# A Mamba-2 and mixture-of-experts block on one core: two gate pairs of in-projection done in the group's own first scan tile

## Chip, core and metric

The kernel runs on one core of one Trainium2 chip, written at the level of the engines' own instruction streams. The metric is device time in microseconds (us) of one execution. One core has TensorE (matmuls), VectorE, ScalarE, GpSimd and SyncE, which here only issues DMAs; each runs its own instructions in order, and semaphores tie them together.

## The reference

The input is 2048 tokens of 512 numbers. A layer norm is followed by two branches whose results are added to the input: a Mamba-2 block and a mixture of 8 experts with the top 2 taken.

```python
xn = _layernorm(x)
zxbcdt = xn @ in_proj_w.T                     # 1024 z, 1280 xBC, 16 dt
xBC = silu(conv_b + sum(conv_w[:, k] * xp[:, k:k + l, :] for k in range(4)))
...                                           # scan over chunks with decays exp(dt * A)
y = (Y_diag + Y_off) + x_heads * D_skip
y = y * silu(z)
y = y * rsqrt(mean(y * y) + EPS) * norm_w
out = x + y @ out_proj_w.T + moe(xn)
```

The gate z enters at one place only: after the scan has given y, y is multiplied by silu(z). The columns xBC are needed from the first step of the scan.

## The kernel before

The experts run first (the trace's first 300 us or so, with layer norm and routing ahead of them); the Mamba part follows. Its 16 tiles of 128 tokens (t = 0 to 15) are scanned one after the other, and two tiles make one group of 256 tokens (g = t // 2; c = t % 2 is the tile's place in it, so "even" tiles have c = 0 and "odd" ones c = 1).

**In-projection** works on a whole group at a time, in 9 pairs of column blocks: `PAIRS` (L150) names five pairs that go through the convolution (`True`) and four gate pairs, the z pairs (`False`). A pair is 24 matmuls of 128 by 256 into one of two PSUM banks, `pi[n % 2]` (`stage_pe`, L1323). A conv pair is then copied to `raw` by ScalarE, which also makes the first tap (`stage_act`, L1262); VectorE adds three taps to each of its two blocks, six instructions (L1297), and after a tanh on ScalarE finishes the pair with one instruction (L1309), which stands in the code of the next pair. A z pair is one tanh on ScalarE (L1278) and one instruction on VectorE (L1303). TensorE may write a bank again when its last reader is done: ScalarE's copy for a conv pair, VectorE's L1303 for a z pair.

**Order.** Group 0's nine pairs are done in a lead-in ahead of tile 0. After that group g + 1's pairs are spread over the two tiles of group g: `TAKEN` (L943) puts pairs 0 to 3 in the even tile and 4 to 8 in the odd one. Group 7 has no group behind it, so tiles 14 and 15 have no pairs.

**A tile on TensorE**: transposes of the tile's x (L1629, L1633), a pair (`stage(0)`), a product for C and B (L1637, behind ScalarE's `btok` copy), a pair (`stage(1)`), the out-projection of the tile before (`project(t - 1)`, 16 matmuls at L1593, and then the sum of squares at L1598, which waits for GpSimd's tree of sums), the first half of the carried state's product (`off(0)`, L1614), a pair (`stage(2)`), `off(1)`, half of the tile's own product (`diag(0)`, L1621), the state update (L1655), `diag(1)`, and what pairs are left (`stage(3)`, `stage(4)`).

**A tile on VectorE**: `xdt` (two instructions, L1494), `cbm` (L1501), the masking of `m` (L1504, 2048 elements), `dec` (L1447) for the next tile, the residual of the tile before, the conv or gate work of the tile's first two pairs, the variance and `decayed(0)` (L1467), the output of the tile before (L1567), `decayed(1)`, `own(0)` (L1476), the third pair's work, the split of x in odd tiles (L1320), `own(1)`, `carry` (L1533), and then the work of the remaining pairs.

**ScalarE and GpSimd** are tied to it so: `dec` on VectorE lets ScalarE do its exponentials (L1360, L1361), four parts of `m` (L1368), and then the square of y of the tile before (L1384); behind that square GpSimd makes the tree of three sums (L1206 to L1210) for which L1598 waits. GpSimd also adds and gates y at a tile's end (L1252, L1255) and makes `xdd` when `xdt` is there (L1226).

All engines run group 0 unrolled, groups 1 to 6 in a loop of two groups a turn, and group 7 unrolled.

Of the kernel before, what the change touches and what calls it, by code (L numbers as in the profile page):

```python
# [36 lines left out]
G = T // 2  # L37
# [107 lines left out]
CR = 1  # L145
# [1 line left out]
SLOT = 2 * GU + 2 * DW  # L147


PAIRS = ((True, 0), (True, 1), (True, 2), (False, 0), (True, 3), (True, 4), (False, 1), (False, 2), (False, 3))  # L150
NP = len(PAIRS)
EARLY = XB * D * 4 + KD * GT * 4 + 384


# [34 lines left out]
def static(i, *values):  # L189
    return isinstance(i, int) and i in values  # L190
# [747 lines left out]
def mamba(nc, low, over, late, wraw, whl, wo, xh0, smalls, hooks, sem, x, w_in, w_out_in, conv_w_in, conv_b_in,  # L938
# [1 line left out]
    NX, NZ = CB // 2, XB // 2  # L940
    y_out, y_done, down, h_lo = experts.y_out, experts.y_done, experts.down, experts.h_lo
    assert NP == NX + NZ
    TAKEN = ((0, 1, 2, 3), (4, 5, 6, 7, 8))  # L943
    with ExitStack() as ctx:
        def pb(name, shape):
            return ctx.enter_context(nc.psum_tensor(name, shape, F32))
# [40 lines left out]
        w_lo = sem("w_lo")  # L987
# [145 lines left out]
        def sync(sp):  # L1133
            sp.wait_ge(down, J + CR)
            sp.wait_ge(y_done, J + CR)
            sp.wait_ge(h_lo, J + 2)
            for i in range(2):
                sp.wait_ge(y_out[i], 16 * ((J + 1 - i) // 2) + 16)

            def load_x(g, par):  # L1140

                sp.dma_start(xl[par][:, :, :].bitcast(F32), xt_d[g]).then_inc(xg_in[par], 16)

            def load_decays(t, c):
                sp.dma_start(m[c][:, :, :], cs_d[t].unsqueeze(0).broadcast_to([P, HEADS, P])).then_inc(bc_in[c], 16)

            def load_decays2(t):
                for half in range(2):
                    sp.dma_start(e2[half * HD:(half + 1) * HD, :, :],
                                 cs_d[t][half * XB:(half + 1) * XB, :].unsqueeze(0).broadcast_to([HD, XB, P])  # L1150
                                 ).then_inc(e2_in, 16)

            def store(t):
                sp.wait_ge(o_done, t + 1 + CR)
                sp.dma_start(out_t[t], o[:, :]).then_inc(o_out, 16)

            sp.wait_ge(w_lo, NP)
            load_decays(0, 0)
            load_x(1, 1)

            def body(g, par):
                for c in range(2):
                    t = g * 2 + c
                    if not static(t, T - 1):
                        sp.wait_ge(ydiag, t * 2 + CR)
                        load_decays(t + 1, 1 - c)
                    if c == 0 and not static(g, G - 2, G - 1):
                        sp.wait_ge(in_full, g * NP + NP + CR)
                        load_x(g + 2, par)
                    elif c == 0 and static(g, G - 2):  # L1170

                        sp.wait_ge(in_full, g * NP + NP + CR)
                        sp.sem_inc(xg_in[par], 16)
                    sp.wait_ge(yadd, t + CR)
                    load_decays2(t)
                    if not static(t, 0):
                        store(t - 1)
                    sp.dma_start(res[:, :], x_t[t]).then_inc(res_in, 16)

            body(0, 0)  # L1180
            body(1, 1)
            with sp.Fori(0, (G - 4) // 2) as i:
                body(i * 2 + 2, 0)
                body(i * 2 + 3, 1)
            body(G - 2, 0)
            body(G - 1, 1)
            store(T - 1)
            sp.wait_ge(o_out, 16 * T + 16)
# [157 lines left out]
        def scalar(act):  # L1346
# [36 lines left out]
                act.wait_ge(ygate, t + 1 + CR)  # L1383
                act.activation(ysq[:, :, :], y[:, :, :], ACT.Square).then_inc(ysqd, 1)  # L1384

            for n in range(NP):
                stage_act(act, 0, n, 0)
                if n == 6:
                    decay_factors(0, 0)
            split_act(act, 1, 1, 0)  # L1390
            kernel_part(0, 0, 0, 1)
# [1 line left out]
            def body(g, par, r):  # L1393
                for c in range(2):
                    t = g * 2 + c
                    taken = TAKEN[c] if not static(g, G - 1) else ()
                    more = not static(t, T - 1)
                    act.wait_ge(btr, t + 1)
                    act.wait_ge(st, t + CR)
                    act.copy(btok[:, :], pk[:, 0, :]).then_inc(btok_done, 1)  # L1400
                    for n in taken[:1]:
                        stage_act(act, g + 1, n, 1 - par)
                    act.wait_ge(e2_in, t * 32 + 32)
                    act.activation(e2[:, :, :], e2[:, :, :], ACT.Exp).then_inc(e2_done, 1)
                    if more:
                        decay_factors(t + 1, 1 - c)
                        kernel_part(t + 1, 1 - c, 0, 4)
                    if not static(t, 0):
                        square(t - 1)
                    for n in taken[1:2]:  # L1410
                        stage_act(act, g + 1, n, 1 - par)
                    if more:
                        kernel_part(t + 1, 1 - c, 1, 4)
                        kernel_part(t + 1, 1 - c, 2, 4)
                    for n in taken[2:3]:
                        stage_act(act, g + 1, n, 1 - par)
                    if more:
                        kernel_part(t + 1, 1 - c, 3, 4)
                    if c == 1 and taken:
                        split_act(act, g + 2, par, r + 1)  # L1420
                    for n in taken[3:]:
                        stage_act(act, g + 1, n, 1 - par)

            by_twos(act, G, body)
            square(T - 1)
# [1 line left out]
        def vector(dve):  # L1427
# [18 lines left out]
                dve.wait_ge(cst_done, t + 1)  # L1446
                dve.tensor_tensor(dec[c][:, :], m[c][:, :, P - 1], cst[c][:, :], ALU.subtract).then_inc(dsub, 1)  # L1447

            for n in range(NP):
                stage_dve(dve, 0, n, 0)  # L1450
                if n == 6:
                    decay_differences(0, 0, 0)
            split_dve(dve, 1, 1)

            def body(g, par):
                for c in range(2):
                    t = g * 2 + c
                    tok = slice(c * P, (c + 1) * P)
                    first = static(t, 0)
                    taken = TAKEN[c] if not static(g, G - 1) else ()  # L1460

                    def decayed(half):

# [43 lines left out]
                        decay_differences(t + 1, g + c, 1 - c)  # L1507
                    if not first:
                        residual(t - 1)
                    for n in taken[:2]:  # L1510
                        stage_dve(dve, g + 1, n, 1 - par)
                    if static(t, T - 1):
                        decayed(0)
                    if not first:
# [4 lines left out]
                        finish(t - 1)  # L1519
                    decayed(1)  # L1520
                    own(0)
                    for n in taken[2:3]:
                        stage_dve(dve, g + 1, n, 1 - par)
                    if c == 1 and taken:
                        split_dve(dve, g + 2, par)
                    own(1)
# [3 lines left out]
                    for half in range(2):  # L1530
# [1 line left out]
                        sl = carry[:, 4 * half:4 * half + 4, :, :].rearrange("p b a d -> p (b a d)")  # L1532
                        dve.tensor_tensor(sl, pxb[half][:, :, :].rearrange("p b l -> p (b l)"), sl,  # L1533
                                          ALU.add).then_inc(cadd, 1)
                    for n in taken[3:4]:
                        stage_dve(dve, g + 1, n, 1 - par)
                    for n in taken[4:]:
                        stage_dve(dve, g + 1, n, 1 - par)

            def residual(t):  # L1540

# [33 lines left out]
        def tensor(pe):  # L1575
            for s in (st, yoff, ydiag, op, ss):
                pe.sem_inc(s, CR)
            for n in range(1, NP):
                pe.wait_ge(w_lo, n + 1)
                stage_pe(pe, 0, n, 0)  # L1580
            pe.wait_ge(prep, 5)
            pe.wait_ge(wo_done, XB)

# [16 lines left out]
            def body(g, par):  # L1600
                for c in range(2):
                    t = g * 2 + c
                    tok = slice(c * P, (c + 1) * P)
                    taken = TAKEN[c] if not static(g, G - 1) else ()

                    def stage(n):
                        for k in taken[n:n + 1]:
                            stage_pe(pe, g + 1, k, 1 - par)

                    def off(half):  # L1610
                        pe.wait_ge(ye, t * 2 + half + CR)
# [108 lines left out]
```

## Time and profile before

| | us |
|---|---|
| median of 3 runs | 784.98 (784.42 to 787.63) |
| the profiled execution | 790.81, span 789.0 |
| TensorE busy | 670.8 (85% of the span) |
| VectorE busy | 527.7 (67%) |
| ScalarE busy | 379.9 (48%) |
| GpSimd busy | 310.6 (39%) |
| lead-in's last matmul until tile 1's x transposes | 328.35 to 355.68 |
| tiles 2 to 13 | 384.3 to 726.5 |
| tiles 14 and 15 | 726.5 to 789.0 |

Times in rows are microseconds from the start of the span. A group of rows on one engine, in order of time, has the start, the length, the engine, the line of the kernel, the operation, the names written and read, and the count; brackets hold the idle time of the engine just before, and the instruction that ended it. PEclk is the clock granted to TensorE as a share of the full one: 1.00 is 2.4 GHz and 0.50 is 1.2 GHz.

### The profile page before, as it was taken

The numbers are of one execution on the slowest core, as the hardware profiler recorded it, in microseconds if no ns is written. First come the engines' busy times: TensorE is split into PE (matmuls) and PEld (weight loads), VectorE is DVE, ScalarE is ACT, GpSimd is POOL, SyncE is SP. The second block draws the span as 40 slices with busy tenths as digits, with TensorE's granted clock in tenths as the row PEclk, the third lists the DMA queues.
The fourth block names the chain that finished last, engine by engine and source line by source line (L and its number), as shares of the span: only waits on it lengthen the run. The fifth ranks groups of instructions, "written<-read, shape, count | busy, mean of one in ns | idle before, by whom it ended". The sixth has DMA issues, their size and how long they took to land.

```text
span 789.0 us, 13831 instructions
## 1 busy us (share of the span) xinstructions
PE 670.8 (85%) x4176; PEld 532.2 (67%) x4177; DVE 527.7 (67%) x1051; ACT 379.9 (48%) x776; POOL 310.6 (39%) x288
## 2 busy tenths in 40 slices
PE   0555446999999987979999999899999899999765
PEld 0233225999999877867877786686787687777432
DVE  4676682443444467678788788678788778787453
ACT  3333112444554465676557466456556546564410
POOL 3345103222222200126465464464555455556441
PEclk9866756999999998999999999999999999999797
DMA  8788102654456623212432343242243242134120
GB/s 246 269 283 287 53 7 70 185 187 120 141 180 178 237 101 147 68 61 65 144 117 63 116 134 99 63 134 83 78 132 107 56 131 106 53 107 133 54 64 29
DMA packets 36072, 96.47 MB, mean 122 GB/s; under 512 B 5376, under 2 KB 9216, under 8 KB 33856
## 3 DMA queue, kind: packets, MB, share of 16 engines
q1 hardware_dynamic: 28304, 67.96, 25.0%
q0 software_dynamic: 7728, 28.05, 13.0%
q8 instruction: 16, 0.26, 0.1%
q14 instruction: 24, 0.20, 0.1%
HBM read 73.06 MB, written 22.94 MB: 122 GB/s over the span
## 4 chain that ended last, share of the span: by engine, by line
PE 51%; issue 15%; DVE 12%; POOL 10%; DMA 7%; ACT 3%; POOLq 0%; DVEq 0%; SPq 0%; ACTq 0%
PE pi L1341 17%; PE pg L879 10%; PE pd L890 6%; PE py L1614 4%; PE po L1593 3%; PE py L1621 3%; DMA xn_d<-xin 3%; DMA xin<-in_x 2%; PE px L864 2%; POOL y L1252 2%; POOL ysq L1206 2%; DVE y L1476 2%; POOL xdd L1226 2%; PE pxb L1655 2%; DVE xs L1297 1%
## 5 line engine op out<-in xcount | busy, mean ns | idle before, releaser
L1341 PE MATMUL pi<-xh,whl 128*128 128x256 f32 x1152 | 169.2, 291 | 9.0 <-ACT raw L1272 4.5
L1341 PEld LDWEIGHTS pi<-xh,whl 128*128 128x128 f32 x1152 | 150.7, 194 | 13.4 <-issue 7.1
L1297 DVE SCALAR_TENSOR_TENSOR xs<-raw,conv_w,xs 128x256 f32<-128x256 f32 x240 | 119.5, 567 | 4.6 <-ACT xs L1275 4.6
L1593 PE MATMUL po<-wo,y 128*128 128x512 f32 x256 | 114.9, 602 | 1.9 <-POOL y L1255 1.9
L1341 PE MATMUL pi<-xl,whl 128*128 128x256 f32 x576 | 93.5, 285 | 0.0
L1593 PEld LDWEIGHTS po<-wo,y 128*128 128x128 f32 x256 | 48.2, 193 | 57.6 <-issue 55.3
L1341 PEld LDWEIGHTS pi<-xl,whl 128*128 128x128 f32 x576 | 79.8, 193 | 0.0
L1368 ACT ACTIVATE m<-m,cst 128x128 f32<-128x128 f32 x256 | 79.4, 388 | 0.5
L879 PE MATMUL pg<-ew,xgh 128*128 x312 | 65.3, 352 | 0.0
L1252 POOL TENSOR_TENSOR y<-y,e 128x1024 f32<-128x1024 f32 x15 | 35.9, 2390 | 66.6 <-DVE y L1476 66.6
L1226 POOL TENSOR_TENSOR xdd<-xdt,dec 128x1024 f32<-128x1024 f32 x15 | 29.1, 1938 | 72.7 <-DVE xdt L1494 72.7
L1206 POOL TENSOR_TENSOR ysq<-ysq 128x512 f32<-128x512 f32 x16 | 22.6, 1412 | 86.4 <-ACT ysq L1384 78.6
L879 PEld LDWEIGHTS pg<-ew,xgh 128*128 128x128 f32 x312 | 53.5, 192 | 0.3
L765 POOL COPY ic<-idx 128x1 uint32 (+1 forms) x39 | 7.2, 183 | 115.3 <-PE px L864 79.1
L1504 DVE TENSOR_TENSOR m<-m,cbm 128x2048 f32<-128x2048 f32 x16 | 51.1, 3194 | 1.7
L768 POOL DMA_INDIRECT xg<-xn_d,ic x39 | 38.1, 977 | 31.7 <-POOL ic L765 31.7
L1278 ACT ACTIVATE zs<-pi 128x512 f32<-128x512 f32 x32 | 19.1, 598 | 63.4 <-PE pi L1341 63.4
L649 PE MATMUL pt<-ident,xin 128*128 128x128 f32 x64 | 15.7, 427 | 39.5 <-DVE xin L423 39.5
L1239 POOL DMA_INDIRECT ya<-y_d,sidx x32 | 40.1, 1254 | 18.0 <-POOL sidx L1234 13.2
L832 DVE SCALAR_TENSOR_TENSOR hg<-th,pg 128x192 f32<-128x192 f32 x39 | 13.8, 354 | 49.9 <-ACT th L788 49.9
L890 PE MATMUL pd<-ew,hh 96*128 x156 | 45.8, 414 | 0.3 <-issue 0.3
L1275 ACT ACTIVATE xs<-raw,conv_b,conv_w 128x256 f32<-128x256 f32 x80 | 43.7, 594 | 1.3
(193 smaller groups left out, 1270.5 us busy)
## 6 DMA issues: line engine op xcount, KB each, us to landing
m<-cs_d SPq DMA_DIRECT2D x16, 1024.0 KB, 4.8
y_d<-yo SPq DMA_DIRECT2D x39, 256.0 KB, 3.3
e<-cs_d SPq DMA_DIRECT2D x32, 256.0 KB, 4.1
gur<-in_w_gu POOLq DMA_DIRECT2D x8, 768.0 KB, 5.2
xin<-in_x SPq DMA_DIRECT2D x8, 512.0 KB, 4.9
xn_d<-xin SPq DMA_DIRECT2D x8, 512.0 KB, 4.8
xt_d<-xt SPq DMA_DIRECT2D x8, 512.0 KB, 3.6
xl<-xt_d SPq DMA_DIRECT2D x8, 512.0 KB, 3.7
```

Source lines behind the costliest of these rows:

```text
L879: mm = pe.matmul(pg[par][:, :], xx[par][:, k, :], of(ww, e, k), start=n == 0, stop=n == 11)
L890: mm = pe.matmul(pd[par][:, :], xx[par][:, k, :], of(ww, e, k), start=n == 0, stop=n == 5)
L1206: pool.tensor_tensor(ysq[:, 0:4, :], ysq[:, 0:4, :], ysq[:, 4:8, :], ALU.add).then_inc(tree, 1)
L1226: pool.tensor_tensor(xdd[:, :, :, :], xdt[:, :, :, :], dec[c][:, :].rearrange("p (a b) -> p b a", a=2).unsqueeze(3) .broadcast_to([P, XB, ...
L1239: pool.indirect_dma_start(ya[n][:, :], None, y_d, bass.IndirectOffsetOnAxis(ap=sidx[:, n:n + 1], axis=0)).then_inc(ya_in[n], 16)
L1252: pool.tensor_tensor(y[:, :, :], y[:, :, :], e2[:, :, :], ALU.add).then_inc(yadd, 1)
L1275: act.activation(xs[par][:, b, :], raw[:, b, 0:GT], ACT.Identity, bias=conv_b[:, b:b + 1], scale=conv_w[:, b, 0:1]).then_inc(tap, 1)
L1297: dve.scalar_tensor_tensor(out=xs[par][:, b, :], in0=raw[:, b, k:k + GT], scalar=conv_w[:, b, k:k + 1], in1=xs[par][:, b, :], op0=ALU.mult ...
L1341: mm = pe.matmul(pi[n % 2][:, h, :], whl[:, n, lo, k, h * P:(h + 1) * P], xx[:, k, :], start=k3 == 0, stop=k3 == 11)
L1368: act.activation(m[c][:, h, :], m[c][:, h, :], ACT.Relu, bias=cst[c][:, h:h + 1], scale=-1.0).then_inc(seg, 1)
L1504: dve.tensor_tensor(m[c][:, :, :], m[c][:, :, :], cbm[:, :].unsqueeze(1).broadcast_to([P, HEADS, P]), ALU.mult).then_inc(m_done, 1)
L1593: mm = pe.matmul(po[:, :], y[:, b, :], wo[:, b, :], start=b == 0, stop=b == XB - 1)
```

## The change

`PAIRS` now has the five conv pairs first (0 to 4) and the four z pairs last (5 to 8). The last two, `OWN = 2`, are no longer done a group ahead: pairs 7 and 8 of group g are done in tile 2g, in the places `stage(0)` and `stage(1)`. Behind them in the same tile come pairs 0, 1, 2 of group g + 1, and pairs 3, 4, 5, 6 in the odd tile. The lead-in does 7 pairs, and tile 14 has group 7's pairs 7 and 8. On SyncE the next x for the split is loaded after the decays `e2` and no longer before, since all nine pairs of the group are now done only in its first tile.

```diff
-PAIRS = ((True, 0), (True, 1), (True, 2), (False, 0), (True, 3), (True, 4), (False, 1), (False, 2), (False, 3))
+PAIRS = ((True, 0), (True, 1), (True, 2), (True, 3), (True, 4), (False, 0), (False, 1), (False, 2), (False, 3))
+OWN = 2
...
-    TAKEN = ((0, 1, 2, 3), (4, 5, 6, 7, 8))
+    def taken_in(g, c):
+        own = [(g, n) for n in range(NP - OWN, NP)] if c == 0 else []
+        ahead = [(g + 1, n) for n in ((0, 1, 2) if c == 0 else (3, 4, 5, 6))] if not static(g, G - 1) else []
+        return own + ahead
...
+                    sp.wait_ge(yadd, t + CR)
+                    load_decays2(t)
                     if c == 0 and not static(g, G - 2, G - 1):
                         sp.wait_ge(in_full, g * NP + NP + CR)
                         load_x(g + 2, par)
...
-                    sp.wait_ge(yadd, t + CR)
-                    load_decays2(t)
...
-            for n in range(NP):
+            for n in range(NP - OWN):
                 stage_dve(dve, 0, n, 0)
-                if n == 6:
+                if n == 5:
                     decay_differences(0, 0, 0)
...
-                    taken = TAKEN[c] if not static(g, G - 1) else ()
+                    taken = taken_in(g, c)
...
-                    for n in taken[4:]:
-                        stage_dve(dve, g + 1, n, 1 - par)
+                    for of, n in taken[4:]:
+                        stage_dve(dve, of, n, par if of is g else 1 - par)
...
-            for n in range(1, NP):
+            for n in range(1, NP - OWN):
                 pe.wait_ge(w_lo, n + 1)
                 stage_pe(pe, 0, n, 0)
+            pe.wait_ge(w_lo, NP)
```

The other uses of `taken` change in the same way on ScalarE, VectorE and TensorE, and ScalarE's lead-in like VectorE's.

VectorE, from the end of tile 0 (the carry) to the first instructions of tile 1; `zs` is a z pair, `xs<-raw` are conv taps, `xs<-tx` finishes a conv pair. Before:

```order
L1533 TENSOR_TENSOR carry<-pxb,carry 128x512 x2
L1303 SCALAR_TENSOR_TENSOR zs_163<-zs_163,pi 128x512
L1309 SCALAR_TENSOR_TENSOR xs_161<-tx_178,xs_161 128x512
L1494 TENSOR_TENSOR xdt<-pxb,dt_tok 128x512 x2
L1501 TENSOR_TENSOR cbm<-pk,tri 128x128
```

and of the change:

```order
L1541 TENSOR_TENSOR carry<-pxb,carry 128x512 x2
L1305 SCALAR_TENSOR_TENSOR xs_161<-raw,conv_w,xs_161 128x256 x6
L1317 SCALAR_TENSOR_TENSOR xs_161<-tx_178,xs_161 128x512
L1305 SCALAR_TENSOR_TENSOR xs_161<-raw,conv_w,xs_161 128x256 x6
L1317 SCALAR_TENSOR_TENSOR xs_161<-tx_179,xs_161 128x512
L1502 TENSOR_TENSOR xdt<-pxb,dt_tok 128x512 x2
L1509 TENSOR_TENSOR cbm<-pk,tri 128x128
```

Two whole conv pairs now stand between the carry of an even tile and `xdt` of the odd one, where one z instruction and the finish of a conv pair stood; it is the same in tiles 2, 4, ..., 12.

TensorE in the same place, from `diag(1)` of tile 0 to the transposes of tile 1; four rows of `pi` are one pair. Before:

```order
L1621 MATMUL py<-m_151,xdt 64x128 x8
L1341 MATMUL pi<-xh_180,whl 128x256 x8
L1341 MATMUL pi<-xl_157,whl 128x256 x4
L1341 MATMUL pi<-xh_180,whl 128x256 x8
L1341 MATMUL pi<-xl_157,whl 128x256 x4
L1629 MATMUL pk<-ident,xs_160 128x128
L1633 MATMUL pxb<-ident,xs_160 128x128 x8
```

and of the change:

```order
L1630 MATMUL py<-m_151,xdt 64x128 x8
L1349 MATMUL pi<-xh_180,whl 128x256 x8
L1349 MATMUL pi<-xl_157,whl 128x256 x4
L1349 MATMUL pi<-xh_180,whl 128x256 x8
L1349 MATMUL pi<-xl_157,whl 128x256 x4
L1349 MATMUL pi<-xh_180,whl 128x256 x8
L1349 MATMUL pi<-xl_157,whl 128x256 x4
L1349 MATMUL pi<-xh_180,whl 128x256 x8
L1349 MATMUL pi<-xl_157,whl 128x256 x4
L1638 MATMUL pk<-ident,xs_160 128x128
L1642 MATMUL pxb<-ident,xs_160 128x128 x8
```

The even tile ends with two pairs where it ended with one; the odd tile has four in all where it had five.

## Rows read from the trace of the kernel before

**Rows 1.** The page, part 1: busy time, share of the span, instructions.
```profile
PE 670.8 (85%) x4176; PEld 532.2 (67%) x4177; DVE 527.7 (67%) x1051; ACT 379.9 (48%) x776; POOL 310.6 (39%) x288
```

**Rows 2.** Busy time by stretch: lead-in, tiles 2, 3, 6 and 14.
```profile
core 0: us, PE busy (x) PEld busy (x) DVE busy (x) ACT busy (x) POOL busy (x), PEclk, DMA share, GB/s
311.00:328.40 17.40, 17.40 (x147) 17.40 (x146) 13.06 (x29) 9.49 (x18) 0.00 (x0) 0.99 0.02 9
384.23:410.55 26.32, 25.89 (x180) 20.13 (x178) 21.27 (x44) 16.00 (x35) 12.68 (x11) 1.00 0.35 106
410.55:440.00 29.45, 28.97 (x203) 22.85 (x202) 24.31 (x43) 16.78 (x35) 17.52 (x13) 1.00 0.32 104
...
495.75:526.50 30.75, 27.84 (x179) 21.49 (x177) 23.54 (x44) 16.44 (x36) 13.08 (x11) 0.94 0.32 97
726.53:750.24 23.71, 19.02 (x84) 11.75 (x82) 11.19 (x18) 9.78 (x23) 10.97 (x10) 0.78 0.24 67
```

**Rows 3.** TensorE in tile 3: start, length, instruction, [idle before <-who].
```profile
411.16 1.09 PE L1633 MATMUL pxb<-ident,xs 128*128 128x128 f32 x8 [0.34 <-DVE carry L1533]
...
418.00 7.03 PE L1593 MATMUL po<-wo,y 128*128 128x512 f32 x16
425.17 0.38 PE L1598 MATMUL pk<-ones,ysq 128*128 128x1 f32 x2
```

**Rows 4.** VectorE, tiles 2, 3 and 4, the same columns.
```profile
409.82 1.28 DVE L1533 TENSOR_TENSOR carry<-pxb,carry 128x512 f32<-128x512 f32 x2
...
411.98 0.93 DVE L1309 SCALAR_TENSOR_TENSOR xs<-tx,xs 128x512 f32<-128x512 f32 x1
412.83 1.27 DVE L1494 TENSOR_TENSOR xdt<-pxb,dt_tok 128x512 f32<-128x512 f32 x2
...
415.76 3.45 DVE L1504 TENSOR_TENSOR m<-m,cbm 128x2048 f32<-128x2048 f32 x1
...
419.32 0.18 DVE L1447 TENSOR_TENSOR dec<-m,cst 128x16 f32<-128x16 f32 x1
...
421.26 6.52 DVE L1297 SCALAR_TENSOR_TENSOR xs<-raw,conv_w,xs 128x256 f32<-128x256 f32 x12
...
461.49 2.46 DVE L1297 SCALAR_TENSOR_TENSOR xs<-raw,conv_w,xs 128x256 f32<-128x256 f32 x6
```

**Rows 5.** ScalarE, tile 3, the same columns.
```profile
421.09 1.04 ACT L1384 ACTIVATE ysq<-y 128x1024 f32<-128x1024 f32 x1
```

**Rows 6.** GpSimd, tile 3, the same columns.
```profile
412.52 2.63 POOL L1255 TENSOR_TENSOR y<-y,zs 128x1024 f32<-128x1024 f32 x1 [0.17 <-POOL y L1252]
415.11 1.95 POOL L1226 TENSOR_TENSOR xdd<-xdt,dec 128x1024 f32<-128x1024 f32 x1
...
424.60 0.52 POOL L1210 TENSOR_TENSOR ysq<-ysq 128x128 f32<-128x128 f32 x1
```

**Rows 7.** Conv taps of tile 3 by line: xcount, ns min/median/max.
```profile
L1297 DVE SCALAR_TENSOR_TENSOR xs<-raw,conv_w,xs x12: 472/478/1493, 421.3 to 427.3; 128x256 f32<-128x256 f32 x12
```

**Rows 8.** VectorE and ScalarE, lead-in and tile 0.
```profile
312.55 2.56 DVE L1297 SCALAR_TENSOR_TENSOR xs<-raw,conv_w,xs 128x256 f32<-128x256 f32 x6 [0.70 <-ACT xs L1275]
...
330.11 1.23 DVE L1320 TENSOR_TENSOR xl<-xl,xh 128x1024 fp32r<-128x1024 f32 x1 [0.25 <-ACT xh L1315]
...
336.61 0.25 ACT L1400 COPY btok<-pk 128x128 f32<-128x128 f32 x1
```

**Rows 9.** TensorE after an idle time: tiles 0, 1, 6 and 14.
```profile
331.39 1.61 PE L1341 MATMUL pi<-xh,whl 128*128 128x256 f32 x8 [1.90 <-DVE xl L1320]
...
347.06 1.16 PE L1614 MATMUL py<-xs,carry 128*128 128x128 f32 x8 [3.16 <-DVE e L1467]
...
355.68 1.09 PE L1633 MATMUL pxb<-ident,xs 128*128 128x128 f32 x8 [0.39 <-DVE carry L1533]
...
512.34 0.38 PE L1598 MATMUL pk<-ones,ysq 128*128 128x1 f32 x2 [2.14 <-POOL ysq L1210]
...
739.07 0.58 PE L1598 MATMUL pk<-ones,ysq 128*128 128x1 f32 x2 [3.42 <-POOL ysq L1210]
```

More of the change, by code:

```diff
@@ L1400, in body @@
                     act.copy(btok[:, :], pk[:, 0, :]).then_inc(btok_done, 1)
-                    for n in taken[:1]:
-                        stage_act(act, g + 1, n, 1 - par)
+                    for of, n in taken[:1]:
+                        stage_act(act, of, n, par if of is g else 1 - par)
                     act.wait_ge(e2_in, t * 32 + 32)
@@ L1409, in body @@
                         square(t - 1)
-                    for n in taken[1:2]:
-                        stage_act(act, g + 1, n, 1 - par)
+                    for of, n in taken[1:2]:
+                        stage_act(act, of, n, par if of is g else 1 - par)
                     if more:
@@ L1414, in body @@
                         kernel_part(t + 1, 1 - c, 2, 4)
-                    for n in taken[2:3]:
-                        stage_act(act, g + 1, n, 1 - par)
+                    for of, n in taken[2:3]:
+                        stage_act(act, of, n, par if of is g else 1 - par)
                     if more:
@@ L1420, in body @@
                         split_act(act, g + 2, par, r + 1)
-                    for n in taken[3:]:
-                        stage_act(act, g + 1, n, 1 - par)
+                    for of, n in taken[3:]:
+                        stage_act(act, of, n, par if of is g else 1 - par)
             by_twos(act, G, body)
@@ L1447, in decay_differences @@
                 dve.tensor_tensor(dec[c][:, :], m[c][:, :, P - 1], cst[c][:, :], ALU.subtract).then_inc(dsub, 1)
-            for n in range(NP):
+            for n in range(NP - OWN):
                 stage_dve(dve, 0, n, 0)
-                if n == 6:
+                if n == 5:
                     decay_differences(0, 0, 0)
@@ L1459, in body @@
                     first = static(t, 0)
-                    taken = TAKEN[c] if not static(g, G - 1) else ()
+                    taken = taken_in(g, c)
                     def decayed(half):
@@ L1509, in body @@
                         residual(t - 1)
-                    for n in taken[:2]:
-                        stage_dve(dve, g + 1, n, 1 - par)
+                    for of, n in taken[:2]:
+                        stage_dve(dve, of, n, par if of is g else 1 - par)
                     if static(t, T - 1):
@@ L1521, in body @@
                     own(0)
-                    for n in taken[2:3]:
-                        stage_dve(dve, g + 1, n, 1 - par)
+                    for of, n in taken[2:3]:
+                        stage_dve(dve, of, n, par if of is g else 1 - par)
                     if c == 1 and taken:
@@ L1534, in body @@
                                           ALU.add).then_inc(cadd, 1)
-                    for n in taken[3:4]:
-                        stage_dve(dve, g + 1, n, 1 - par)
-                    for n in taken[4:]:
-                        stage_dve(dve, g + 1, n, 1 - par)
+                    for of, n in taken[3:4]:
+                        stage_dve(dve, of, n, par if of is g else 1 - par)
+                    for of, n in taken[4:]:
+                        stage_dve(dve, of, n, par if of is g else 1 - par)
             def residual(t):
@@ L1603, in body @@
                     tok = slice(c * P, (c + 1) * P)
-                    taken = TAKEN[c] if not static(g, G - 1) else ()
+                    taken = taken_in(g, c)
                     def stage(n):
-                        for k in taken[n:n + 1]:
-                            stage_pe(pe, g + 1, k, 1 - par)
+                        for of, k in taken[n:n + 1]:
+                            stage_pe(pe, of, k, par if of is g else 1 - par)
                     def off(half):
```

## Prediction

> **What bounds the kernel.** The page first: TensorE is busy for 670.8 of 789.0 us [rows 1]. Busy time by stretch says where the rest lies. In the steady part (tiles 2 to 13) TensorE has nothing to give: tile 2 is 26.32 us long and 25.89 busy, tile 3 29.45 and 28.97, at a granted clock of 1.00; tile 6, with one longer wait, 30.75 and 27.84 at 0.94; tile 14, without pairs, 23.71 and 19.02 at 0.78 [rows 2]. So a pair moved out of the steady part, or into idle time of tile 0 or tile 14, is worth up to its own length: in the lead-in 147 matmuls took 17.40 us, so the 24 of a pair take 24 x 17.40 / 147 = 2.84 us [rows 2]. TensorE's work is the same in sum before and after. The question is what the new order does to its waits.
>
> The second thing to read is how late the other engines are. In tile 3 (T = 410.55, its first transpose) `project` starts at 418.00 and lasts 7.03 us, to 425.03, and the sum of squares behind it starts at 425.17 [rows 3]. What releases that one is a chain over three engines: `xdt` on VectorE at 412.83, the masking of `m` from 415.76, `dec` done at 419.32 + 0.18 = 419.50 [rows 4]; the square on ScalarE at 421.09 [rows 5]; GpSimd's tree, whose last sum ends at 424.60 + 0.52 = 425.12 [rows 6]. GpSimd ends 0.05 us ahead of the matmul that waits for it. So the odd tiles hold two limits that are level: TensorE's own order and the chain xdt, m, dec, square, tree. The chain has 425.12 - 419.50 = 5.62 us from the end of `dec` to the end of the tree.
>
> **What the change gains.** (a) Lead-in. TensorE has two pairs fewer, 5.68 us, but tile 0 also needs the five conv pairs finished, which now come in a row. VectorE's third starts at 312.55 and takes 2.56 [rows 8] plus some 0.6 for a finish; three of these, a z and a finish end at 312.55 + 3 x 3.1 + 1.2 = 323.1. TensorE is done at 322.7, so tile 0 starts at about 323.1 and not 328.35: 5.2 us. (b) Tile 0 gives most of it back. ScalarE's copy `btok`, at 336.61 now [rows 8], comes some 4.5 us earlier, 332.1; pair 8 is behind it on TensorE, and pair 0 of the next group, which writes the same bank, waits for VectorE to read pair 8, behind the masking of `m`, at about 338.9. From there 3 pairs (8.52), off, diag, state update and diag (4.9) and about 1 us for half rate lead to 353.3, where tile 1 starts at 355.3 now (355.68 less its wait of 0.39, [rows 9]): 2.0 us are left. (c) From tile 1 to tile 13 seven odd tiles lose a pair and six even ones gain one: -2.84. (d) Tile 14 takes two pairs. There TensorE waited 3.42 us for the tree and then ran at half rate [rows 9]. With the pairs, `cbm` and `m` come 2.2 us later and the tree ends at about 14.5 us into the tile, as `project` does (it starts at 7.5, lasts 7.0); without the idle time I take the rest at full rate, 6.8 us, so 21.3 in place of 23.71: -2.4. Together -2.0 - 2.84 - 2.4 = -7.2 us.
>
> **What it costs in each odd tile.** Pairs 1 and 2, both conv pairs, are the last things an even tile does on TensorE, and their VectorE work stands ahead of `xdt` of the odd tile. Where `xdt` starts at T + 2.3 now [rows 4], it needs:
> The low end: pair 2's last matmul is at T, its copy and first activation let VectorE begin at T + 1.3; six taps 2.46 [rows 4] and the finish 0.6 give T + 4.4. That holds if pair 1 costs nothing.
> The high end: pair 1's taps can begin at T - 1.5, and GpSimd gates y of the even tile from about T - 1.0 to T + 1.4 (2.4 us; it comes earlier against T since the even tile is a pair longer). Taps and finish read two SBUF tensors, and they stall under a GpSimd tensor operation: one tap took 1493 ns against a median of 478 [rows 7], a finish took 0.93 under the gate, and the masking of `m` 3.45, and ended 2.15 us behind the end of `xdd`, which had started first [rows 4, 6]. If the gate holds the taps to its end, four taps of pair 1 follow it: 1.4 + 1.9 = T + 3.3, finish 3.95, six taps 6.45, finish 7.1, and with a tap that is in the way of the gate, T + 7.3.
> Between the ends: twelve taps took 6.52 us over a tree of about 2.9 us, and two sixes alone would be 4.92, so 1.6 of 2.9 was lost; by this share the gate costs 1.3 and not 2.4, and `xdt` starts at about T + 6.3. I take T + 7.3, since the 1.45 us sum, the longest of that tree, blocked a single tap for 1.0 and the gate is longer than it.
>
> The Trainium skill, page "SBUF — State Buffer", section "Who interferes with whom", says that VectorE with two SBUF inputs and a GpSimd instruction that reads SBUF exclude each other for a whole instruction, and the one that comes second is blocked. By that rule the gate costs its full 2.4 us, the high end; the 1493 ns tap agrees.
>
> From `xdt` on: 1.3 us, then `xdd` 1.95, which holds `m`, 2.15 more for `m`, 0.35 for `dec`, 5.62 to the end of the tree: 11.4 in all, so T + 18.7. TensorE, with no wait at its transposes, is through `project` at T + 0.1 + (425.03 - 411.16) = T + 14.0. It waits 4.7 us, against 0.5 and 0.1 at the transposes and the sum of squares now: +4.1. Behind it come off(0) and a pair, 3.8 us, and off(1), which needs VectorE's decayed(0). VectorE, with residual (1.75), twelve taps (6.7) and now two finishes after `dec`, reaches that at about T + 23.3: at full rate TensorE waits 0.8 more. If the idle time lowers the clock, that stretch takes some 1.7 us longer instead: waits of 1.90, 2.14 and 3.42 were followed by matmuls at half rate, one of 3.16 was not [rows 9]. I take +0.8. So +4.9 per odd tile and, from a slightly later start of the even tiles' xdt, 0.1 per even one. Seven odd tiles (1 to 13): 34.3, six even ones: 0.6.
>
> ScalarE has the same instructions as before, with `btok` behind a tanh that waits for pair 1's taps: it is there at about T + 4.0, just when TensorE comes to L1637: nothing. SyncE: the wait for the nine pairs, in the middle of the even tile now, holds back the load of x, which is split a tile later, and behind it the store, which waits for `o` longer anyway: nothing; the `e2` load no longer stands behind it, and its exponential is not on the chain. DMA traffic is the same.
>
> **The sum.** 34.3 + 0.6 - 7.2 = +27.7 us. The profiled execution took 790.81 us, 5.8 above the median of the runs; on it this gives 818.5, and on the median of 784.98 it gives 812.7. I forecast 812.
>
> **Rivals.**
> 1. The stall is small: `xdt` at T + 4.4, the low end. The tree ends at T + 15.8, TensorE waits 1.9 (+1.3), and 0.5 more at off(1): 7 x 1.8 + 0.6 - 7.2 = +6.0, 791. For it: the wait is too short to cost clock. Against it: it needs the gate not to disturb six taps.
> 2. Faster: the chain does not bind at all, and only the -7.2 is left: 778. It decides at `xdt` by T + 2.6 (14.0 less 11.4); pair 2's own six taps alone forbid that by 1.8 us unless TensorE has some other slack in the odd tile. Against it too: the chain is level with TensorE today.
> 3. The clock: a wait of 4.7 us is followed by more than one stretch at half rate, as in tile 14 (0.78 over the tile, [rows 2]). Then each odd tile costs 1.7 us more: 824.
> 4. No difference: rival 1 with a smaller wait, the seven odd tiles costing 1 us each: 785.
>
> **How the numbers follow.** Forecast 0.55, rival 1 0.20, rival 3 0.08, rival 2 0.09, rival 4 0.08. The range reaches from rival 1 to rival 3 and leaves out rivals 2 and 4, 0.17: 790 to 826. About 0.5% is what a measurement of this kernel can tell from no change: faster 0.09, within it 0.08, slower 0.83.
>
> **What will show it.** In the changed profile: tile 1 starts near 353; in every odd tile up to 13 TensorE is idle by 4 to 5 us ahead of the sum of squares, released by GpSimd; `xdt` of odd tiles starts 7 us after the first transpose; a group (even and odd tile) takes about 60.5 us where it takes 55.8; tile 14 is near 21.3 us at a granted clock near 1. I would be wrong if VectorE's taps at the tile's edge ran undisturbed (a wait under 2 us), if the odd tile's chain hid behind TensorE, or if the half rate came in most tiles and for long.

## The result: 3.2% slower, 810.6 us

| | before | after |
|---|---|---|
| median of 4 runs, us | 784.7 (780.3 to 787.6) | 810.63 (806.38 to 812.38) |
| ratio | | 1.0319, 95% interval 1.0272 to 1.0365 |
| profiled execution, us | 790.81, span 789.0 | 806.38, span 804.7 |
| start of tile 0 | 328.35 | 314.97 |
| tile 2, tile 3 | 26.32, 29.45 | 29.40, 32.56 |
| tile 4, tile 5 | 26.20, 29.37 | 29.33, 31.74 |
| tile 6, tile 10 | 30.30, 30.62 | 30.16, 30.12 |
| tile 14 | 23.71 | 21.78 |

812 was forecast. In the profiled execution of the changed kernel the part ahead of the Mamba lead-in, which the change doesn't touch, took 7.87 us less (the lead-in's third pair starts at 297.92, before at 305.79). So I compare from there on: the lead-in and the tiles took 23.6 us longer (15.7 by the spans, and 7.9), where the working had 27.7. Executions over 1.5% behind a kernel's fastest are left out of the ratios below but not of the medians (with the shorter gate they are three of ten, and its median without them is 791.93).

Busy time by stretch, the columns as in [rows 2]: the end of the lead-in, tiles 2, 3, 5, 6 and 14.

```profile
297.92:314.97 17.05, 16.59 (x120) 16.42 (x121) 16.06 (x38) 11.02 (x20) 0.00 (x0) 0.86 0.47 166
376.11:405.51 29.40, 28.63 (x204) 22.87 (x203) 18.88 (x35) 14.98 (x33) 17.47 (x13) 1.00 0.38 125
405.51:438.07 32.56, 28.54 (x179) 22.46 (x178) 28.58 (x53) 17.87 (x37) 10.82 (x11) 0.90 0.23 70
467.40:499.14 31.74, 27.57 (x179) 21.49 (x178) 28.64 (x53) 17.85 (x37) 10.86 (x11) 0.95 0.22 66
499.14:529.30 30.16, 28.92 (x204) 22.81 (x202) 19.67 (x35) 15.00 (x33) 17.51 (x13) 1.00 0.38 124
745.00:766.78 21.78, 20.23 (x131) 14.28 (x129) 12.65 (x22) 10.87 (x25) 13.57 (x11) 1.00 0.30 92
```

Tile 3 has a pair less than before (179 matmuls, where [rows 2] has 203) and takes 3.1 us longer; it is the worst of the odd tiles, the other six up to 13 take 2.1 to 2.4 us longer at clocks of 0.95. TensorE is idle for 4 us of it, and its clock is at half rate for part of the rest. TensorE in tile 3 (T = 405.51):

```profile
412.83 7.03 PE L1602 MATMUL po<-wo,y 128*128 128x512 f32 x16
423.72 0.59 PE L1607 MATMUL pk<-ones,ysq 128*128 128x1 f32 x2 [3.86 <-POOL ysq L1218]
424.17 2.06 PE L1623 MATMUL py<-xs,carry 128*128 128x128 f32 x8
425.88 2.05 PE L1349 MATMUL pi<-xh,whl 128*128 128x256 f32 x8
427.73 1.05 PE L1349 MATMUL pi<-xl,whl 128*128 128x256 f32 x4
428.59 1.28 PE L1349 MATMUL pi<-xh,whl 128*128 128x256 f32 x8
...
430.18 1.05 PE L1623 MATMUL py<-xs,carry 128*128 128x128 f32 x8
```

The sum of squares, which followed the out-projection at once in [rows 3], waits 3.86 us for GpSimd's last sum; in the other odd tiles up to 13 it is 3.67 to 3.92. Behind it eight matmuls of a pair take 2.05 us, and 1.28 and less once the clock is back. VectorE and GpSimd over the same edge say why the sum is late:

```profile
404.11 4.59 DVE L1305 SCALAR_TENSOR_TENSOR xs<-raw,conv_w,xs 128x256 f32<-128x256 f32 x6 [1.49 <-ACT xs L1283]
408.62 0.68 DVE L1317 SCALAR_TENSOR_TENSOR xs<-tx,xs 128x512 f32<-128x512 f32 x1
409.23 2.45 DVE L1305 SCALAR_TENSOR_TENSOR xs<-raw,conv_w,xs 128x256 f32<-128x256 f32 x6
411.60 0.68 DVE L1317 SCALAR_TENSOR_TENSOR xs<-tx,xs 128x512 f32<-128x512 f32 x1
412.20 1.27 DVE L1502 TENSOR_TENSOR xdt<-pxb,dt_tok 128x512 f32<-128x512 f32 x2
...
417.89 0.18 DVE L1455 TENSOR_TENSOR dec<-m,cst 128x16 f32<-128x16 f32 x1
...
427.52 0.67 DVE L1475 TENSOR_TENSOR e<-py,e 128x512 f32<-128x512 f32 x1
```

```profile
404.06 2.38 POOL L1263 TENSOR_TENSOR y<-y,zs 128x1024 f32<-128x1024 f32 x1 [0.17 <-POOL y L1260]
413.70 1.93 POOL L1234 TENSOR_TENSOR xdd<-xdt,dec 128x1024 f32<-128x1024 f32 x1 [7.26 <-DVE xdt L1502]
...
423.16 0.51 POOL L1218 TENSOR_TENSOR ysq<-ysq 128x128 f32<-128x128 f32 x1
```

Pair 1's six taps take 4.59 us and pair 2's 2.45. The first six began at 404.11, 0.05 us after GpSimd's gate. The six by line (ns minimum, median, maximum) show that one of them, of 2616 ns, paid for all of it; it ended 0.29 us behind the gate:

```profile
L1305 DVE SCALAR_TENSOR_TENSOR xs<-raw,conv_w,xs x6: 472/472/2616, 404.1 to 408.2; 128x256 f32<-128x256 f32 x6
```

So `xdt` starts at T + 6.7, where it stood at T + 2.3 [rows 4], and the tree ends at 423.67, 11.5 us behind the start of `xdt`.

### The profile page after: what moved, and what is told of

The parts are those of the page before. It is cut to its first block, busy times and chain, and to the rows that moved or that the text cites. A ratio compares the mean times of both kernels' runs of the same rounds, so it can differ in the third digit from the quotient of the medians.

```text
span 804.7 us, 13829 instructions
## 1 busy us (share of the span) xinstructions
PE 672.9 (84%) x4176; PEld 537.5 (67%) x4177; DVE 534.2 (66%) x1051; ACT 379.8 (47%) x776; POOL 300.1 (37%) x288
## 4 chain that ended last, share of the span: by engine, by line
PE 45%; issue 18%; DVE 15%; POOL 7%; ACT 6%; DMA 6%; DVEq 0%; POOLq 0%; ACTq 0%; SPq 0%
PE pi L1349 14%; PE pg L880 9%; PE pd L891 6%; PE po L1602 3%; DVE xs L1305 3%; PE py L1623 3%; DMA xin<-in_x 2%; DMA xn_d<-xin 2%; PE px L865 2%; POOL ysq L1214 2%; POOL xdd L1234 2%; ACT m L1376 2%; PE py L1630 2%; PE pxb L1664 2%; DVE xs L1317 1%
## 5 line engine op out<-in xcount | busy, mean ns | idle before, releaser
L1349 PE MATMUL pi<-xh,whl 128*128 128x256 f32 x1152 | 175.4, 298 | 5.0 <-ACT raw L1280 4.5
L1349 PEld LDWEIGHTS pi<-xh,whl 128*128 128x128 f32 x1152 | 156.9, 202 | 7.9 <-issue 7.7
L1305 DVE SCALAR_TENSOR_TENSOR xs<-raw,conv_w,xs 128x256 f32<-128x256 f32 x240 | 125.1, 586 | 12.5 <-ACT xs L1283 12.4
L1349 PE MATMUL pi<-xl,whl 128*128 128x256 f32 x576 | 95.8, 290 | 0.0
L1349 PEld LDWEIGHTS pi<-xl,whl 128*128 128x128 f32 x576 | 82.3, 199 | 0.0
L1512 DVE TENSOR_TENSOR m<-m,cbm 128x2048 f32<-128x2048 f32 x16 | 57.2, 3575 | 1.7
L1255 POOL TENSOR_TENSOR carry<-carry,cd 128x1024 f32<-128x1024 f32 x15 | 29.0, 1934 | 36.6 <-PE py L1623 36.6
L650 PE MATMUL pt<-ident,xin 128*128 128x128 f32 x64 | 14.7, 405 | 32.4 <-DVE xin L424 32.4
```

What stands on the lines that cost most here:

```text
L1305: dve.scalar_tensor_tensor(out=xs[par][:, b, :], in0=raw[:, b, k:k + GT], scalar=conv_w[:, b, k:k + 1], in1=xs[par][:, b, :], op0=ALU.mult ...
L1349: mm = pe.matmul(pi[n % 2][:, h, :], whl[:, n, lo, k, h * P:(h + 1) * P], xx[:, k, :], start=k3 == 0, stop=k3 == 11)
L1512: dve.tensor_tensor(m[c][:, :, :], m[c][:, :, :], cbm[:, :].unsqueeze(1).broadcast_to([P, HEADS, P]), ALU.mult).then_inc(m_done, 1)
```

## Experiments

The theory: conv taps ahead of the odd tile's `xdt` are the loss, the gate makes them worse, and the half rate after the wait is a part of its own. Rivals: the loss comes from doing gate pairs in their own tile; or the half rate costs nothing, since VectorE is late for `off(1)` anyway. Times are medians; ratios are against the runs of the kernel before in the same series (784.2 to 785.4).

### The own gate pairs last in the even tile

```diff
-        return own + ahead
+        return ahead + own
```

with the waits for banks and for the group's last pair set to the new order.

> The change is kept (two gate pairs of a group are done in its own even tile, the lead-in has 7 pairs, tile 14 has two), but within the even tile the order is turned round: pairs 0, 1, 2 of the next group stand in the first three places, and the group's own gate pairs 7 and 8 come last. So no convolution taps stand ahead of xdt of the odd tile, only two gate pairs. My theory (the loss is the late xdt of odd tiles, because two conv pairs with their taps stand ahead of it): the wait of 3.9 us ahead of the sum of squares falls below 1 us in odd tiles, the half rate behind it is gone, odd tiles take 29.4 less 2.84 = 26.6 us and not 31.75, so 7 x 5.1 = 36 us less than the change's own 810, less what tile 14 loses: about 775 to 782 us, faster than the kernel before. Rival (the loss comes from doing gate pairs in the group's own tile at all, by the banks or the masking ahead of L1311): it stays at 800 to 812 us.

809.15 us, ratio 1.0346 (1.0274 to 1.0418): the time is in the rival's range (800 to 812). The trace says otherwise. VectorE in tile 5 (T = 472.48):

```profile
473.92 1.28 DVE L1516 TENSOR_TENSOR xdt<-pxb,dt_tok 128x512 f32<-128x512 f32 x2
...
483.12 0.18 DVE L1466 COPY cst<-cs_tok 128x16 f32 x1 [2.60 <-DMA m<-cs_d]
483.33 0.18 DVE L1469 TENSOR_TENSOR dec<-m,cst 128x16 f32<-128x16 f32 x1
```

SyncE's queue in the same tile:

```profile
472.83 0.35 SPq L1158 DMA_DIRECT2D xl<-xt_d  x1
473.38 1.15 SPq L1171 DMA_DIRECT2D out<-o  x1
474.72 0.34 SPq L1194 DMA_DIRECT2D res<-in_x  x1
475.34 0.33 SPq L1161 DMA_DIRECT2D m<-cs_d  x1
475.77 1.15 SPq L1165 DMA_DIRECT2D e<-cs_d  x2
```

`xdt` was early, at T + 1.4, as the theory had it. But SyncE waits for the group's last pair before it loads the next x, and this pair was now at the even tile's very end. The loads of the decays stood behind that wait, were issued at 475.34 and 475.77, and `dec` waited 2.60 us for the one at 475.34 (in tile 13, where no x is loaded any more, the exponential on ScalarE waited 2.51 us for the `e` load instead). My edit had taken one wait away and made another, on a queue that I had not looked at.

### The same, with the x load behind the decays on SyncE

```diff
                         load_decays(t + 1, 1 - c)
                     sp.wait_ge(yadd, t + CR)
                     load_decays2(t)
-                    if c == 0 and not static(g, G - 2, G - 1):
+                    if c == 1 and not static(g, G - 2, G - 1):
                         sp.wait_ge(in_full, full_at(g, NP - 1) + CR)
                         load_x(g + 2, par)
```

> As the kernel with the own gate pairs last in the even tile, with one more move: SyncE's wait for the group's nine pairs and the load of the next x behind it stand in the odd tile, behind the loads of the decays, and no longer in the even tile ahead of them. In that kernel's trace the odd tiles' xdt was early (T + 1.4 in tile 5), but dec then waited 2.60 us for the load of the decays, which SyncE issued only when pair 8 was done, and in tile 13 the exponential ahead of dec's waited 2.5 us for the e2 load. Theory (the taps cost was gone and a late DMA issue had taken its place): odd tiles wait under 1 us ahead of the sum of squares and take 26.6 to 27.7 us in place of 27.7 to 33.4, so 7 x 4 us less than 809: 775 to 785 us. Rival (the loads are late because of their own traffic, or another wait of that order comes up): odd tiles stay above 29 us and the time above 795.

773.57 us, ratio 0.9861 (0.9804 to 0.9919), so faster than the kernel before. Tiles 4, 5 and 6, then TensorE in tile 5 (T = 458.22):

```profile
429.12:458.22 29.10, 28.89 (x203) 22.90 (x202) 23.34 (x46) 16.59 (x36) 16.78 (x12) 1.00 0.31 102
458.22:484.72 26.50, 26.02 (x179) 19.95 (x178) 22.62 (x41) 16.12 (x34) 12.84 (x11) 1.00 0.34 101
484.72:515.10 30.38, 29.14 (x204) 22.80 (x203) 24.52 (x46) 16.61 (x36) 16.61 (x12) 1.00 0.32 104
```

```profile
472.22 0.38 PE L1621 MATMUL pk<-ones,ysq 128*128 128x1 f32 x2
472.46 1.14 PE L1637 MATMUL py<-xs,carry 128*128 128x128 f32 x8
...
476.75 1.16 PE L1637 MATMUL py<-xs,carry 128*128 128x128 f32 x8 [0.34 <-DVE e L1489]
```

The odd tiles take 26.4 to 26.5 us: the 29.4 of before less one pair of 2.84. The even tiles take 29.1 us, the 26.2 of before and one pair. So gate pairs in their own tile, at the even tile's end, cost no more than their own length. In the places of the change, `stage(0)` and `stage(1)`, they were not run without the conv pairs at the tile's end; its even tiles are 0.2 us longer than these.

### One part of the change alone: the order of PAIRS

The kernel before with the new `PAIRS` line and nothing else of the change, groups 1 to 6 written out.

> The kernel before, groups 1 to 6 written out, with one part of the change alone: PAIRS in the new order (five conv pairs first, then four gate pairs). All nine pairs stay one group ahead, 0 to 3 in the even tile and 4 to 8 in the odd one, so nothing is done in the group's own tile, and TensorE has the same work in each tile as before. What changes is that the even tile ends with a conv pair (3) and not a gate pair. Theory (conv taps ahead of the odd tile's xdt are the cost, one pair of them a part of it): xdt of odd tiles moves from T + 2.3 to between T + 4.8 (six taps of 2.46 us and a finish behind pair 3's activation, undisturbed) and T + 7.1 (held by GpSimd's gate, which stands at T + 1.9 to T + 4.6), TensorE waits 2 to 4.5 us ahead of the sum of squares, and seven odd tiles cost 2 to 6 us each: 792 to 818 us against 778 of the written-out kernel before. Rival (the loss needs the gate pairs done in their own tile): 776 to 781.

814.31 us, ratio 1.0339 (1.0285 to 1.0392), against 778.08 for the written-out kernel before (below): 36 us (the two are from different series, whose kernels before are 1.0 us apart) for a change of order that leaves the number of pairs in each tile as it was. VectorE and GpSimd in tile 5 (T = 475.36):

```profile
476.81 4.81 DVE L1297 SCALAR_TENSOR_TENSOR xs<-raw,conv_w,xs 128x256 f32<-128x256 f32 x6 [0.86 <-ACT xs L1275]
...
482.15 1.28 DVE L1495 TENSOR_TENSOR xdt<-pxb,dt_tok 128x512 f32<-128x512 f32 x2
```

```profile
477.30 2.46 POOL L1255 TENSOR_TENSOR y<-y,zs 128x1024 f32<-128x1024 f32 x1
```

One conv pair with the gate on top of it puts `xdt` at T + 6.8, as late as two pairs did in the change, where the gate meets only the first. The wait ahead of the sum of squares is 3.40 to 3.54 us. Tiles 3, 5 and 11:

```profile
414.78:449.10 34.32, 30.50 (x204) 24.39 (x202) 26.86 (x43) 16.77 (x35) 17.11 (x13) 0.95 0.27 87
475.36:508.07 32.71, 28.80 (x204) 22.69 (x202) 26.93 (x43) 16.84 (x35) 17.06 (x13) 1.00 0.28 95
655.68:691.10 35.42, 31.61 (x204) 25.49 (x203) 26.95 (x43) 16.78 (x35) 17.08 (x13) 0.90 0.27 87
```

Tile 5 stayed at the full clock and is 3.5 us longer than the 29.2 of the written-out kernel before, so there the wait costs its own length and no more. Tiles 3 and 11 have the same wait and another 1.6 and 2.7 us at clocks of 0.95 and 0.90.

### A shorter gate

```diff
-                    pool.tensor_tensor(y[:, :, :], y[:, :, :], zs[par][:, :, c * P:(c + 1) * P],
+                    pool.tensor_tensor(y[:, 0:1, :], y[:, 0:1, :], zs[par][:, 0:1, c * P:(c + 1) * P],
```

> The changed kernel with GpSimd's gate (y times silu of z) done on one of its eight blocks only, so that 7/8 of the gating is left out and GpSimd's 2.4 us instruction becomes about 0.3 us. Nothing else is different. Theory (the gate holds up pair 1's taps, 4.59 us for six in tile 3 where six take 2.45 undisturbed): six taps of pair 1 take about 2.6 us, xdt of odd tiles starts near T + 4.7 in place of T + 6.7, the wait ahead of the sum of squares falls from 3.9 to about 1.9 us, and with less or no half rate behind it the odd tiles lose 2 to 3.7 us each: 784 to 797 us. Rival (pair 2's taps alone set xdt and the gate hides behind them, or the taps are slow by themselves): xdt stays within 0.5 us of T + 6.7 and the time within 4 us of 810.

793.42 us, ratio 1.0102 (1.0055 to 1.0149): 17 us less than the changed kernel. The kernel leaves out seven eighths of the gating. Over the same edge (T = 411.21, in an execution of 798.71 us) VectorE and GpSimd have

```profile
409.82 2.69 DVE L1305 SCALAR_TENSOR_TENSOR xs<-raw,conv_w,xs 128x256 f32<-128x256 f32 x6 [1.49 <-ACT xs L1283]
...
416.00 1.28 DVE L1502 TENSOR_TENSOR xdt<-pxb,dt_tok 128x512 f32<-128x512 f32 x2
```

```profile
409.78 0.47 POOL L1263 TENSOR_TENSOR y<-y,zs 128x128 f32<-128x128 f32 x1 [0.17 <-POOL y L1260]
```

The taps fell from 4.59 to 2.69, `xdt` moved to T + 4.8, and the wait to 2.13 to 2.54. A gate shorter by 1.9 us took 1.9 us off the chain. The rest, T + 4.8 against T + 2.3, is for the most part pair 2's own taps and finish (3.1 us, where one finish of 0.9 stood). This is close to rival 1 of the prediction (`xdt` at T + 4.4, 791).

### TensorE kept busy through the wait

```diff
+                for _ in range(fill):
+                    pe.matmul(pk[:, 3, :], ident[:, :], ident[:, :], start=True, stop=True)
                 pe.wait_ge(tree, t * 3 + 6)
```

The dummies stand in all eight odd tiles, also in tile 15, where there is no wait to fill.

> The changed kernel with 26 small matmuls (identity by identity, 128 x 128, into an unused part of a PSUM bank) on TensorE in odd tiles, between the out-projection and the wait for the tree of squares: about 3.5 us of work by the transposes' 0.136 us each, so that TensorE is busy through the wait instead of idle. Theory (the idle time of 3.9 us is one part of the loss, the half rate behind it another): the granted clock stays full behind the wait, the pair's 24 matmuls there take 2.8 us and not 4.5, off(1) starts 1.7 us earlier, and seven odd tiles give 7 x 1.7 = 12 us: about 798 us. Rival (VectorE's decayed sets off(1) anyway, at about T + 23 to 24): 0 to 1 us per odd tile, 803 to 810 us. If the dummies overrun the tree they cost up to 0.2 us a tile.

819.92 us, ratio 1.0453 (1.0399 to 1.0507), where about 798 was expected: a miss, and not even in the direction, with two causes. I had taken 0.136 us for a small matmul from the transposes, but the trace has two rows for each dummy, and the 26 took 5.97 us, 1.8 beyond the tree. And in tiles 5 and 9, ahead of the loop's turn, there was something new:

```profile
501.51 0.63 PE L1349 MATMUL pi<-xl,whl 128*128 128x256 f32 x4
506.20 0.47 PE L1640 MATMUL pk<-ident,xs 128*128 128x128 f32 x1 [4.07 <-issue]
```

TensorE stood for 4.07 and 4.38 us with nothing to wait for. Even so the other odd tiles were 31.7 to 31.9 us long, as without the dummies, for all the 1.8 us of overrun: the clock gave that back. The same with 15 dummies and no loop:

> As the changed kernel written out, with 15 small matmuls (identity by identity) in the wait of odd tiles. 26 of them took 5.9 us in the run with the loop, so 15 take 3.4 and end before the tree does. There TensorE went on at full rate: off(1) at T + 24.0 although the dummies overran the tree by 1.8 us, against T + 24.7 in the changed kernel. Theory (half rate is 1.7 to 2 us of each odd tile's loss): odd tiles take 29.9 to 30.2 us in place of 31.75, 7 x 1.7 = 12 us less than the written-out changed kernel: about 797. Rival (VectorE sets off(1): with taps at 4.15 us its decayed(0) came at T + 22.1 in that run, so it would not): 0 to 0.5 us per odd tile, 806 to 809.

793.42 us, ratio 1.0108 (1.0051 to 1.0166), against 807.88 for the same without the dummies (below): 14.5 us, where 12 was expected. TensorE in tile 5 (T = 465.05):

```profile
482.99 0.38 PE L1610 MATMUL pk<-ones,ysq 128*128 128x1 f32 x2 [0.34 <-POOL ysq L1218]
483.23 1.14 PE L1626 MATMUL py<-xs,carry 128*128 128x128 f32 x8
484.12 1.17 PE L1349 MATMUL pi<-xh,whl 128*128 128x256 f32 x8
...
487.52 1.16 PE L1626 MATMUL py<-xs,carry 128*128 128x128 f32 x8 [0.34 <-DVE e L1476]
```

The tree is no earlier, but eight matmuls of a pair take 1.17 us behind it, not 2.05. The odd tiles take 30.4 us instead of 31.3 to 32.4 (mean 32.0) and the even ones 28.75 instead of 29.35. The two traces are 16.8 us apart from tile 0 on: the seven odd tiles give 11.4 us of it, the six even ones 3.6 (VectorE's carry ahead of them starts at T - 0.9 and not T - 0.3) and tiles 14 and 15 1.2. Tile 0, ahead of the first dummy, is 0.6 us shorter too, which is not the dummies' doing. So some 14 us of the changed kernel's time are the clock and what follows from it, and not the waiting. VectorE's part at `off(1)` is 0.34 us.

### The loop of two groups a turn written out

```diff
-            by_twos(eng, G, lambda g, par, r: body(g, par))
+            for g in range(G):
+                body(g, g % 2)
```

and the like on ScalarE and SyncE.

> The kernel before with groups 1 to 6 of the Mamba part written out on every engine in place of the loop of two groups a turn. Theory (in the kernel before tiles 6 and 10, the first of a loop's turn, are 30.3 and 30.6 us long against 26.2 in tiles 4, 8 and 12 because VectorE stands for 3.7 to 4 us at the loop's branch, which ends in a wait of 2.1 to 2.5 us and a half rate on TensorE): each loses about 4 us, so 785 becomes about 777. Rival (these two tiles are long for another reason, such as the DMA traffic or the half rate alone): within 2 us of 785.

> The changed kernel with groups 1 to 6 written out in place of the loop. In the kernel before this took tiles 6 and 10 from 30.3 and 30.6 to 26.4 us. In the changed kernel these two are 30.1 us long against 29.3 of tiles 4, 8 and 12, so theory: 0.8 us each, 1.6 in all, 809 us; the change costs 809 - 778 = 31 us against the written-out kernel before, close to the 27.7 + 2.9 x 2 - ... of the per-tile sum (my forecast had taken the gain and loss of tiles 6 and 10 for those of the others). Rival (the loop's turn costs the changed kernel as much as the one before, hidden somewhere): 802 us, and the change costs 24 us as with the loop.

778.08 us, ratio 0.9946 (0.9904 to 0.9988), and 807.88 us, ratio 1.0274 (1.0207 to 1.0340). Written out, the change costs 29.8 us by the medians and not 25.9. VectorE at the turn, the kernel before (T = 495.57), then the changed one (T = 499.14):

```profile
500.75 1.29 DVE L1494 TENSOR_TENSOR xdt<-pxb,dt_tok 128x512 f32<-128x512 f32 x2 [3.66 <-issue]
```

```profile
503.20 1.29 DVE L1502 TENSOR_TENSOR xdt<-pxb,dt_tok 128x512 f32<-128x512 f32 x2 [2.48 <-issue]
```

In the kernel before, VectorE stands 3.66 us at the turn, `xdt` comes at T + 5.2, and this ends in the wait of 2.14 us ahead of the sum of squares in tile 6 that [rows 9] show. Written out, tile 6 takes 26.39 us and not 30.30, and tile 10 26.38 and not 30.62:

```profile
492.41:518.80 26.39, 25.87 (x179) 20.14 (x178) 21.24 (x44) 16.00 (x35) 12.42 (x11) 1.00 0.34 108
```

In the changed kernel the stand is 1.2 us shorter, `xdt` is at T + 4.1, the wait is 0.48 us and the clock stays full. There, writing it out changed tile 6 from 30.16 to 29.40 us. Against this the odd tiles were up to 0.7 us longer than in the version with the loop, at clocks of 0.89 to 0.95, and the total moved by 2.8 us only, which the spread of the runs covers (804.3 to 811.3, and 806.4 to 812.4).

### Own pairs last, written out

> The kernel with own gate pairs last and the x load in the odd tile, with groups 1 to 6 written out in place of the loop: the version that should beat both. Theory: 1.5 to 8 us less than the same with its loop, 770 to 778 us, at or below the 778 of the written-out kernel before, since the change's own gain (lead-in 5.5, tile 14 about 2, one pair of 2.84 in the odd tiles) is no longer eaten by the chain of odd tiles, less what tile 0 gives back (3) and what even tiles 2 to 12 give (the gate pair's bank waits for VectorE's masking). Rival (the order is limited by VectorE in even tiles, 29.7 us in place of 29.3): 780 to 786, no gain over the written-out kernel before.

772.68 us, ratio 0.9829 (0.9778 to 0.9880), the fastest here, though from its version with the loop (773.57) it can't be told apart. Even tiles take 29.1 us, odd ones 26.4, and tiles 6 and 10 29.16. Against the written-out kernel before (778.08) the gain is 5.4 us by the medians, which come from different series.

## Why the prediction was right, step by step

| step | forecast | measured |
|---|---|---|
| lead-in | -5.2 | -5.5 |
| tile 0 | +3.2 | +3.1 |
| one even tile (pair of 2.84 and 0.1) | +2.9 | +3.1 |
| one odd tile (4.9 less 2.84) | +2.1 | +2.4 |
| tiles 6 and 10 | as the other even ones | -0.1 and -0.5 |
| tile 14 | -2.4 | -1.9 |
| tile 15 | 0 | -0.8 |
| from the third pair to the end | +27.7 | +23.6 |

**The chain was right and carried the forecast.** Tile 1 starts at 344.76, with the 7.87 us of the part ahead at 352.6, for 353. The chain's length from `xdt` to the end of the tree was 11.5 us for 11.4. Pair 1's taps began at T - 1.4 for T - 1.5, and the gate held them, as the high end had it. The share that I had taken from the twelve taps over the tree (1.3 us of a 2.4 us gate) would have been wrong; the single tap of 1493 ns [rows 7] was the better row.

The Trainium skill, page "SBUF — State Buffer", section "Who interferes with whom", lets a VectorE instruction with two SBUF inputs and a GpSimd instruction that reads SBUF exclude each other for a whole instruction. The tap of 2616 ns agrees with this: it began 0.05 us behind the gate and ended 0.29 us behind the gate's end (404.11 + 2.62 = 406.73, and 404.06 + 2.38 = 406.44).

**Two terms of the odd tile were mis-sized and made up for each other.** The wait was forecast at 4.7 us and is 3.9. `xdt` is 0.6 us earlier than forecast, T + 6.7 for T + 7.3: the gate ended at T + 0.9 and not T + 1.4, and it started ahead of the tap, where the high end had a tap in the way of the gate; `project` ends 0.3 us later (T + 14.3). The aftermath was forecast at 0.8 us. The odd tile is 5.2 us longer than 29.4 less 2.84; with 3.9 less the 0.5 of waits of before that leaves 1.8. I had a choice of two causes for it, VectorE's `decayed(0)` or the half rate, and took the smaller price. VectorE came to `decayed(0)` at T + 22.0 and not T + 23.3, and the run with 15 dummies shows that the half rate is the one that counts. So rival 3 (more clock) was true in part, and so was a sign of being wrong that the prediction had named: matmuls at half rate followed the wait in all seven odd tiles, at clocks of 0.95, and 0.90 in tile 3. The working itself gave 60.8 us for a group (55.8 and 4.9 and 0.1), not the 60.5 that it printed; tiles 2 and 3 took 61.96 and tiles 4 and 5 61.07.

**Tiles 6 and 10 were the step that failed.** I read the row of tile 6 in [rows 9] only as an example of a wait followed by half rate, and let these tiles grow like the others. In the kernel before they are 4 us longer than tile 4 by VectorE's stand at the loop's turn. The change adds a pair there too, but the stand is 1.2 us shorter, and the wait and the half rate behind it nearly go; this pays for the pair, and the two tiles together are 6.5 us below the forecast. The written-out kernels, where no tile has a stand, show what this hid. By their traces they are 33.7 us apart from the lead-in's third pair on (807.6 less 300.8, and 776.0 less 302.9), 6.0 more than the 27.7: the odd tiles cost 2.8 us each and not 2.1, and tile 14 gives 0.8 and not 2.4. So the forecast's nearness is in part luck: too little for the odd tiles' clock and too much for tiles 6 and 10 stood against each other. By the medians, the difference was 25.9 us with the loop and 29.8 without, 1.8 below the working's 27.7 and 2.1 above it. Why the stand is shorter in the changed kernel no run tells; it was 2.45 to 2.73 us in all four kernels with own pairs where VectorE has one. But the question why tile 6 took 30.30 us and tile 4 26.20, at the same work, was there to be asked, and these two tiles should have had a range of their own.

**Tile 14** fell short by 0.5 us: the wait for the tree went and the clock stayed full, as forecast, but the carried state's product at L1623 still waits 0.78 us for VectorE, as before, and I had counted that as gone. Why tile 15 is 0.8 us shorter was not tried.

**Rival 2** (778: the chain does not bind, and the gains are left) is what the own pairs at the even tile's end made true, at 773.6. The gains of the working were real; the conv pairs ahead of `xdt` cost more than they brought.

## What to carry to other kernels

When work moves across a tile's edge, look at what the engine that is not the bottleneck does first in the next tile: here the even tile's end took two gate pairs at no cost beyond their length, and two conv pairs there, whose vector instructions stand in front of `xdt`, made the kernel 3% slower. Then price what moves by what runs beside it on the partner engine, and the idle time that it makes on TensorE twice, once for the wait and once for the clock behind it. When a fix doesn't help, open the trace before believing the rival: the number of the first try spoke against a theory that was right, and a DMA issue behind a moved wait was the reason.

## What the runs showed that I had not expected

- A loop's turn is not free, and the stand can show on another engine: VectorE stood for 3.66 us before and 2.48 after at the turn, and TensorE, which showed no such stand in either, stood for 4.07 and 4.38 us once its loop's body held 52 matmuls more (26 in each of the two odd tiles). There VectorE waited for TensorE (4.19 us in tile 6), so that a stand of its own would not show. No kernel with the loop written out has such a stand (26 dummies were not run so). What the engine does in that time no run here shows.
- Waits of the same length on TensorE, in tiles with the same instructions, are followed by half rate or not: 3.54 us in tile 5 and 3.47 in tile 11 of the kernel with only `PAIRS` changed, at clocks of 1.00 and 0.90, 2.7 us apart.
- Dummy matmuls in waits of 3.7 us, seven times in the run, made the whole kernel 14.5 us faster, although an eighth batch in tile 15 filled no wait and put its sum of squares 3.1 us later (T + 16.5 for T + 13.4).
